# Sums of q's squares: turned and added on VectorE, with one small product between two heads of the output projection

## The reference, cut to what matters

```python
q = (hidden_states @ Wq.T).reshape(bsz, q_len, H, HD).transpose(0, 2, 1, 3)   # 32 batches x 64 rows, 32 heads of 128
...
var = jnp.mean(xf * xf, axis=-1, keepdims=True)          # over the 128 elements of a head
q = xf * jax.lax.rsqrt(var + EPS)                        # times a weight per element
scores = jnp.einsum('bhqd,bhkd->bhqk', q, k) * scale     # 64 x 64 for each batch and head
probs = softmax(scores + mask)
out = jnp.einsum('bhqk,bhkd->bhqd', probs, v) ...  @ Wo.T
```

## Time and profile before

| | |
|---|---|
| median of 3 runs | 1417.54 us (1417.51 to 1418.62) |
| profiled execution, its span | 1417.8 us |
| TensorE busy | 1405.3 us, 99% of the span |
| VectorE busy | 850.8 us, 60% |
| ScalarE busy | 514.2 us, 36% |
| GpSimd busy | 359.5 us, 25% |
| granted TensorE clock | 1.00 |

### The profile page before, as it was taken

One profiled execution on the slowest core, in us unless ns is written; L12 is line 12 of the kernel. 1 busy time (PEld: TensorE's weight loads), 2 busy tenths in 40 slices (PEclk: granted clock), 3 DMA queues, 4 the chain that ended last, 5 costly groups with the idle time before them and its releaser, 6 DMA issues.

```text
span 1417.8 us, 26787 instructions
## 1 busy us (share of the span) xinstructions
PE 1405.3 (99%) x9135; PEld 1124.3 (79%) x9136; DVE 850.8 (60%) x1807; ACT 514.2 (36%) x1117; POOL 359.5 (25%) x374
## 2 busy tenths in 40 slices
PE   9999999999999999999999999999999999999998
PEld 7888887778787787878787878787878888777777
DVE  6444447666666666666666666565678746243359
ACT  5333344333343334333333333333334331222242
POOL 1122223121212121211112121212122101366646
PEclk9999999999999999999999999999999999999999
DMA  7544331111111111111111111111123244554548
GB/s 224 180 124 141 126 116 42 38 35 38 42 37 34 38 41 39 34 37 41 39 33 43 38 41 31 47 32 42 45 79 97 97 149 164 192 194 163 162 149 297
DMA packets 91230, 125.48 MB, mean 89 GB/s; under 512 B 7184, under 2 KB 57360, under 8 KB 90896
## 3 DMA queue, kind: packets, MB, share of 16 engines
q1 hardware_dynamic: 83632, 99.70, 22.3%
q0 software_dynamic: 7520, 24.65, 5.2%
HBM read 86.84 MB, written 37.49 MB: 88 GB/s over the span
## 4 chain that ended last, share of the span: by engine, by line
PE 80%; DVE 2%; issue 1%; DMA 0%; ACT 0%; POOL 0%; DVEq 0%; ACTq 0%
PE ps L592 19%; PE ps L594 18%; PE ps L593 18%; PE ps L978 6%; PE ps L679 5%; PE ps L721 4%; PE ps L994 3%; PE ps L687 2%; PE ps L706 2%; PE ps L973 1%; DVE acc L1878 1%; DVE acc L1885 1%; PE ps L1025 1%; PE ps L891 1%; PE ps L729 0%
## 5 line engine op out<-in xcount | busy, mean ns | idle before, releaser
L489 POOL CAST vth<-vt 128x256 fp32r<-128x256 f32 x64 | 25.4, 396 | 629.6 <-PE ps L721 618.0
L1483 DVE TENSOR_TENSOR al<-ps,ah 128x256 fp32r<-128x256 f32 x256 | 96.0, 417 | 116.3 <-ACT ah L1165 116.3
L1165 ACT CAST ah<-ps 128x256 fp32r<-128x256 f32 x256 | 83.6, 384 | 194.8 <-PE ps L594 188.4
L1477 DVE TENSOR_TENSOR acc<-ps,acc 128x512 f32 (+1 forms) x128 | 87.9, 687 | 109.0 <-PE ps L594 109.0
L592 PE MATMUL ps<-hT,w0h 128*128 128x512 f32 (+1 forms) x384 | 152.2, 396 | 0.0
L594 PE MATMUL ps<-hT,w0h 128*128 128x512 f32 (+1 forms) x384 | 149.9, 390 | 0.0
L593 PE MATMUL ps<-hT,w0l 128*128 128x512 f32 (+1 forms) x384 | 149.5, 389 | 0.0
L483 POOL TENSOR_TENSOR qr<-qv,mhalf 128x8 f32<-128x8 f32 x64 | 105.1, 1642 | 83.4 <-DVE qv L1492 82.3
L1134 ACT COPY qs<-ps 128x512 f32<-128x512 f32 x128 | 75.2, 587 | 120.9 <-PE ps L594 120.9
L1143 ACT ACTIVATE pb<-pb 128x256 f32<-128x256 f32 x128 | 48.3, 418 | 166.3 <-DVE pb L1510 166.2
L592 PE MATMUL ps<-w0l,ah 128*128 128x512 f32 x256 | 103.0, 402 | 0.0
(11 more groups left out here) (238 smaller groups left out, 3079.0 us busy)
## 6 DMA issues: line engine op xcount, KB each, us to landing
wraw<-in_w_att SPq DMA_DIRECT2D x64, 256.0 KB, 2.6
vbuf<-vo SPq DMA_DIRECT2D x16, 512.0 KB, 3.3
kbuf<-ko SPq DMA_DIRECT2D x16, 512.0 KB, 3.8
kt<-kbuf SPq DMA_DIRECT2D x32, 256.0 KB, 2.9
vt<-vbuf SPq DMA_DIRECT2D x64, 128.0 KB, 2.0
wgu<-in_w_gu SPq DMA_DIRECT2D x4, 2048.0 KB, 8.1
y<-ybuf SPq DMA_DIRECT2D x16, 512.0 KB, 6.2
xt<-in_x SPq DMA_DIRECT2D x16, 256.0 KB, 4.0
```

Source lines behind the costliest of these rows:

```text
L1165: act.copy(ah[:, bp, :, b2, :], pv_view(bp, b2)).then_inc(a_hi, 1)
L1477: dve.tensor_tensor(dst, PS[6 + bp][:], dst, ALU.add).then_inc(acc_done, 1)
L1483: dve.tensor_tensor(al[:, bp, :, b2, :], pv_view(bp, b2), ah[:, bp, :, b2, :], ALU.subtract).then_inc(a_lo, 1)
```

## The change

The squares are no longer summed by ones on TensorE. VectorE turns each half of `sq` (128 by 512) in 32 by 32 blocks into `sqT` (`turn_squares`) and adds 32 neighbours (`sum_squares`), which leaves 16 numbers per partition and half, each the sum over a quarter of the head. One float32 product of 128 by 128 constants (`fold`: ones where the partition modulo 32 agrees) by these 32 columns adds over the quarters' partitions, VectorE picks with a 0/1 table (`quarter`) and adds epsilon, and a reduction over 4 gives `qv`. The product moves from behind `scores` to between heads 1 and 2 of `project_out(1)`. In VectorE's step the new instructions stand before `a_rest(i - 1, 0)`, and `slice_lo` of an even step moves into the odd step behind it. The tables are made in the first stage. The steps written out by hand get the same edits; the diff is cut to its core.

```diff
@@ tiles, constants, semaphores
-            sst = sb("sst", [P, 8, 32], F32, a)
+            ssg = sb("ssg", [P, 8, 4], F32, a)
+            sqs = sb("sqs", [P, 2, 2, 8], F32, a)
-            ones32 = sb("ones32", [P, 32], F32, a)
+            sqT = sb("sqT", [P, 16, 32], F32, a)
+        fold1 = sb("fold1", [P, 32])
+        fold = sb("fold", [P, 4, 32])
+        quarter = sb("quarter", [P, 4])
+        sq_turned, sq_part, fold_ok = sem("sq_turned"), sem("sq_part"), sem("fold_ok")
...
@@ gpsimd
-            pool.wait_ge(hT_lo, NT)
-            pool.memset(ones32[:], 1.0).then_inc(acc_zero, 1)
@@ tensor
             def q_sums(j):
-                pe.wait_ge(q_sq, 2 * j + 2)
-                for r in range(4):
-                    s0 = 32 * (r % 2)
-                    mm = pe.matmul(PS[2][32 * r:32 * r + 32, 0:256], ones32[:], sq[:, r // 2, :, s0:s0 + 32],
-                                   start=True, stop=True)
-                mm.then_inc(ss_done, 1)
+                pe.wait_ge(sq_part, 2 * j + 2)
+                pe.matmul(PS[2][:, 0:32], fold[:].rearrange("p a j -> p (a j)"), sqs[:].rearrange("p h r b -> p (h r b)"),
+                          start=True, stop=True).then_inc(ss_done, 1)
...
             def outputs(r, w_before, w_o, o_ready=None):
                 pe.wait_ge(acc_done, 2 * r + 1)
-                project_out(1, w_before, (0, 1, 2, 3))
+                project_out(1, w_before, (0, 1))
+                q_sums(r + 2)
+                project_out(1, w_before, (2, 3))
...
                 scores(d + odd, 1 - odd)
-                q_sums(i + 1)
                 if last:
+                    pe.wait_ge(q_sq, 2 * i + 4)
                     transpose_h2(2, 0)
...
             scores(0, 0)
-            pe.wait_ge(acc_zero, 2)
-            q_sums(0)
+            pe.wait_ge(fold_ok, 4)
             def opening():

                 for i in range(2):
                     for h in range(2):
                         pe.wait_ge(q_sq, 2 * i + 1 + h)
                         q_head(h, 1 - i, i, W[0]).then_inc(q_done, 1)
+                        if h == 0:
+                            q_sums(i)
                     pe.wait_ge(s_scaled, i + 1)
-                    pe.wait_ge(ss_turned, i + 1)
                     scores(i, 1 - i)
-                    q_sums(i + 1)
...
                 q_head(0, 1, 1, W[0]).then_inc(q_done, 1)
+                q_sums(2)
                 probs_v(0, 0)
...
                 scores(1, 1)
-                q_sums(3)
@@ scalar
             def squares(h, j):
-                act.wait_ge(ss_done, j + 1)
+                act.wait_ge(sq_turned, 2 * j + 1 + h)
@@ vector
+            dve.wait_ge(ident_ok, 2)
+            dve.tensor_reduce(fold1[:], ident[:].rearrange("p (a j) -> p j a", a=4), AX, ALU.add).then_inc(fold_ok, 1)
+            dve.tensor_reduce(quarter[:], ident[:].rearrange("p (a j) -> p a j", a=4), AX,
+                              ALU.add).then_inc(fold_ok, 1)
+            dve.wait_ge(fold_ok, 2)
+            dve.tensor_copy(fold[:], fold1[:].unsqueeze(1).to_broadcast([P, 4, 32])).then_inc(fold_ok, 2)
...
+            def turn_squares(j, h):
+                if not isinstance(j, int) or 2 * j + h > 0:
+                    dve.wait_ge(sq_part, 2 * j + h)
+                dve.wait_ge(q_sq, 2 * j + 1 + h)
+                dve.transpose(sqT[:].rearrange("p n i -> p (n i)"), sq[:, h].rearrange("p b s -> p (b s)")).then_inc(
+                    sq_turned, 1)
+            def sum_squares(j, h):
+                dve.wait_ge(sq_turned, 2 * j + 3 + h)
+                dve.tensor_reduce(sqs[:, h].rearrange("p r b -> p b r"), sqT[:].rearrange("p (b r) i -> p b r i", r=2), AX, ALU.add).then_inc(sq_part, 1)
+            def squares_summed(j, h):
+                turn_squares(j, h)
+                sum_squares(j, h)
...
-                dve.transpose(sst[:].rearrange("p b r -> p (b r)"), PS[2][:, 0:256]).then_inc(ss_turned, 1)
+                dve.scalar_tensor_tensor(out=ssg[:].rearrange("p b q -> p q b"),
+                                         in0=PS[2][:, 0:32].rearrange("p (q b) -> p q b", q=4),
+                                         scalar=HD * EPS, in1=quarter[:].unsqueeze(2).to_broadcast([P, 4, 8]),
+                                         op0=ALU.add, op1=ALU.mult).then_inc(ss_turned, 1)
                 dve.wait_ge(ss_turned, j + 1)
-                dve.tensor_scalar(qv[:], sst[:, :, 0], HD * EPS, None, ALU.add).then_inc(q_var, 1)
+                dve.tensor_reduce(qv[:], ssg[:], AX, ALU.add).then_inc(q_var, 1)
@@ vector, dve_step
                 i = 2 * d + odd
+                turn_squares(i + 1, 0)
                 if odd:
                     probs_lo(i, 1)
+                sum_squares(i + 1, 0)
+                if odd:
+                    slice_lo(i - 1, w, sl - 1)
                 if complete[0] is not None:
                     residual(complete[0], 1)
+                squares_summed(i + 1, 1)
                 a_rest(i - 1, 0)
...
                 softmax(i + 1, while_root, while_exp)
-                slice_lo(i, w, sl)
+                if odd:
+                    slice_lo(i, w, sl)
...
             rest_first(range(4, 8))
+            for h in range(2):
+                squares_summed(0, h)
             softmax(0)
...
             def opening():
+                for h in range(2):
+                    squares_summed(1, h)
                 softmax(1, lambda: probs_lo(0, 0), lambda: None)
                 slice_lo(0, W[1], 0)
+                for h in range(2):
+                    squares_summed(2, h)
                 softmax(2, lambda: probs_lo(1, 1, 6), lambda: a_rest(0, 0))
...
             i = STEPS - 2
             h2T_rest(0, 2)
             h2T_rest(1, 3)
+            squares_summed(i + 1, 0)
             residual(7, 1)
+            squares_summed(i + 1, 1)
             a_rest(i - 1, 0)
```

More of the change, by code:

```diff
@@ L157, in build @@
             pb = sb("pb", [P, 8, S], F32, a)
-            sst = sb("sst", [P, 8, 32], F32, a)
+            ssg = sb("ssg", [P, 8, 4], F32, a)
+            sqs = sb("sqs", [P, 2, 2, 8], F32, a)
+            sb("below_vth", [P, 192], F32, a)
             v_hi = sb("vth", [P, 2, HD], F32R, a)
@@ L818, in opening @@
                 pe.wait_ge(s_scaled, 3)
-                pe.wait_ge(ss_turned, 3)
                 scores(1, 1)
-                q_sums(3)
                 pe.wait_ge(acc_done, 4)
@@ L1367, in _ @@
             dve.sem_inc(kn_done, 2)
+            dve.sem_inc(sq_turned, 2)
             dve.sem_inc(a_lo, 4)
@@ L1577, in opening @@
                 slice_lo(1, W[1], 1)
-                dve.wait_ge(acc_zero, 3)
+                dve.wait_ge(acc_zero, 2)
                 add_out(2, 0, 0)
@@ L1651, in _ @@
             i = STEPS - 3
+            turn_squares(i + 1, 0)
             probs_lo(i, 1)
+            sum_squares(i + 1, 0)
+            slice_lo(i - 1, W[0], NC - 4)
             statistics(0)
             residual(5, 1)
+            squares_summed(i + 1, 1)
             a_rest(i - 1, 0)
```

## The result

The change made the kernel slower: 1423.42 us median of six runs (1421.39 to 1424.83) against 1417.92 of six runs of the kernel before, ratio 1.0034 [1.0023, 1.0046]. A second set gave 1422.67 and 1418.28, 1.0029 [1.0019, 1.0038]. The forecast was 1410 us, faster. Each run's time is about 1.7 us above its span; the two profiled executions of the changed kernel have spans of 1419.9 and 1419.2, 2.1 and 1.4 us above the 1417.8 of before. They lie at the lower end of its runs, and the 1417.8 at the upper end of those of before, whose median span is 1416.0 to 1416.5 in the later sets.

A forecast was written before the change was run, and what follows sets the result against it. The prediction took TensorE, busy 99% of the span, as the bound. Its terms, -23.1 + 1.5 + 7.5 + 4.9 + 1.9 = -7.3 us off the median 1417.54, gave 1410 us, range 1398 to 1423.

The forecast's parts named there:

- What goes from TensorE: Old sums behind the scores: removing them gives TensorE back 0.57 us a step, at least 0.16.
- rival 5: The 0.41 us standstill behind the scores belongs to the change of tile width and stays: 1436 us, chance 0.05.
- What TensorE gets: Small float32 product between split products: two unhidden weight loads, 0.21 us a step, bounds 0.05 and 0.45.
- Ordinary steps, even: `project_out(0)` waits for `probs_lo` behind the new sums: 0.05 us in each of 29 steps, +1.5 us.
- The margin is nil: Even steps: the chain from small product to `project_out(0)` takes 1.56 us, and TensorE gets there after 1.57.
- rival 2: The tight even step decides: chain 0.5 us longer with slow small instructions, +14, 1424 us, chance 0.09.
- Opening: First softmaxes: TensorE waits 7.5 us more, in gaps of about 2.8, 3.5 and 2.5; step 2's transposes 5.8 later.
- Rival 3: TensorE's clock falls in the opening's new gaps: +4 with the waits that follow, 1414 us, chance 0.11.
- Late steps, step 62: VectorE lacks room: steps 58 to 61 cost +4.9 us, step 62 and the start of 63 +1.9.
- VectorE comes to them later by about as much: Steps 59 and 61: tiles of x queue behind the later `wraw` load, but VectorE is later too; cost 0.
- signs of being wrong: Ordinary pairs shorten by under 0.5 us, TensorE waits in each even step, or the opening loses under 4 us.

The follow-up runs named there:

- e4: Changed kernel, but in even steps VectorE makes the low half of the turned probabilities before it waits for the small product: 1417.18 us.
- e3: Changed kernel with the two longest TensorE gaps of the opening filled with 40 and 48 unused bf16 products: 1418.12 us.
- e8: Changed kernel with old sums in steps 0 to 2 and 60 to 63, and e4's edit in the other even steps: 1405.87 us.
- e11: e8 with the low halves of the weight slices back at the end of their own steps from step 58 on: 1401.82 us.
- e13: Changed kernel with only the low halves of the weight slices back at the end of their own steps from step 58 on: 1418.64 us.
- e1: The changed kernel run again with no edit, as the base for other runs: 1422.7 us.
- e7: Changed kernel with the opening reordered: small product earlier, first half of the next squares summed inside the softmax: 1417.55 us.
- e10: Changed kernel with the small product in one pass, its operands written as float32r: 1414.03 us.
- e2: Changed kernel with steps 0 to 2 summed the old way, the other 61 steps the new way: 1410.77 us.
- e12: e11 with the small product in one pass, its operands written as float32r: 1395.61 us.

## Why the prediction was wrong

Its own terms, added up to the scores of step 63, give -7.0 us (opening 5.8 + 0.57, as its fourth old sum stands behind the scores of step 3; 56 intervals -18.8; late steps +5.4). The table has +2.6. The 9.6 us between them, by the prediction's steps:

- *What goes from TensorE*: right. 0.57 us came back, so rival 5 is out. Of the rule on mode switches (the Trainium skill, TensorEngine Tiling (Array Packing), Key Properties) no run here shows a price beyond the wait for the last tile.
- *What TensorE gets*: the direct price of two bare loads was right (0.22 against 0.21). Put at nothing were the products behind it, which follow a little further apart: 0.265 in all, 0.055 more. Over the 56 intervals from step 3 to 59 that is 3.1 us.
- *Ordinary steps, even*: **the step that failed most plainly.** "The margin is nil" was priced at 0.05. The chain from the small product to `project_out(0)` took 1.70 us instead of 1.56, and 26 of the 28 even intervals lost 0.18 against the odd ones: 26 x 0.13 = 3.4 us more. It was rival 2's place (0.18 us against its 0.5). e4 shows that the order made it, not VectorE's load: the input of `probs_lo` is there before the small product is.
- *Opening*: the transposes of step 2 come 8.7 us later (250.99 against 242.27) instead of 5.8; 2.9 us more. The gaps came as forecast. e3 shows that 2.2 us of the loss in these profiles are the clock. Rival 3 was a separate case with a chance of 0.11, but its condition, idle gaps of 2.5 to 3.5 us, stood in the forecast itself: it belonged into the sum. The Trainium skill, TensorE: Matmul & The Clock Gate, part 1, says that an idle TensorE goes back to 1.2 GHz; the windows agree (0.78 to 0.87 with gaps, 1.00 in e3 without), but gaps of 2.61 us in e4 and 2.67 us in e8 passed without the fall.
- *Late steps, step 62*: 4.6 us net, forecast 6.8 less the gains there (4 x 0.36), 5.4: right in size by 0.8, which is partly luck. About half comes from a term set at 0, the moved `slice_lo`: "VectorE comes to them later by about as much" did not hold (e8, e11, e13).
- Not foreseen: two stalls in steps 24 and 40 (1.3 us together), below.

3.1 + 3.4 + 2.9 + 1.3 - 0.8 = 9.9, against 9.6. Two of the prediction's own signs of being wrong came true: pairs of ordinary steps shortened by 0.43 us, under 0.5, and TensorE waited in each even step but two.

The medians stand 3.4 us further apart than the first profiles (5.5 against 2.1): the profiled execution of the changed kernel took 1421.6 us, 1.8 under its median, and that of before has a span some 1.6 above what its median of 1417.92 gives.

## What to carry to other kernels

Where one engine is busy 99% of the time, work taken from it is worth only what no new wait gives back: price each new wait at its tightest place, per step and not on average, and move whatever already has its input ahead of the wait. A scheme that pays in the steady state need not be used at the start and the end; keeping the old one there was worth 9 us at the start and, with the weight slices back in their own steps, 4.6 at the end, of 1418. A transfer queued behind another one inherits the lateness of whatever frees the first one's buffer.

## What was not expected of the hardware

A float32 product of 32 columns between long ones costs 0.27 us, in one pass 0.125 (0.57 less the 0.445 won): the price goes by the pass. Behind waits of 2.60 and 3.35 us TensorE ran about 3 us at half clock in the changed kernel; behind 2.61 us (e4) and 2.67 us (e8) it did not. A wait of that length may cost the clock or not.

VectorE, twice in the changed kernel, starts step 24's and step 40's first turn late, at the place where its outer loop goes round. ScalarE, VectorE and the DMA queues from 552.90 to 555.40:
```profile
551.98 0.60 ACT L1139 ACTIVATE sq<-ps 128x512 f32<-128x512 f32 x1
```
```profile
555.40 0.71 DVE L1499 STREAM_TRANSPOSE sqT<-sq 128x512 f32<-128x512 f32 x1 [2.22 <-ACT sq L1139]
```
```profile
q14 instruction: 1, 0.01, 1.3%
```
The row names ScalarE's squares, but those of the first half were there at 552.58, and in the even step shown above the first turn follows without a gap (720.34). What does run in the gap is a load on the DMA queue for instructions, 8 KB at 553.33 for 0.53 us; there is another at 776.12, ahead of the stall of step 40 (2.18 us). The nine kernels with these two stalls (changed, e1, e3 to e7, e10, e13) all have such loads in both gaps. The other five (before, e2, e8, e11, e12) have no load on q14 between 500 and 970 us, and no such stall. e11 loses some 2 us at the same steps, but there it is TensorE that starts late (0.58 and 0.97 us), shortly after long loads (2.11 and 1.99 us) on the other instruction queue, q8. Loads on q14 at other places, 574.38 for one, show no such stall. So VectorE most likely waited for its own instructions there; that is not shown, as no run moved the code alone.
